# Rotary attention: the maximum and position term of four heads in one pass of 32-row products

## The reference, cut to what matters

```python
q = (x @ Wq).reshape(b, l, H, HD).transpose(0, 2, 1, 3)      # H = 16, HD = 64
k = (x @ Wk).reshape(b, l, KV, HD).transpose(0, 2, 1, 3)     # KV = 4, each for 4 heads
...
q = q * cos + _rotate_half(q) * sin
k = k * cos + _rotate_half(k) * sin
attn = jnp.einsum('bhqd,bhkd->bhqk', q, k) / math.sqrt(HD)
rel = (pos[None, :] - pos[:, None]).astype(x.dtype)
attn = attn + slopes[None, :, None, None] * rel[None, None, :, :]
attn = jax.nn.softmax(attn, axis=-1)
out = jnp.einsum('bhqk,bhkd->bhqd', attn, v)
...
return out @ Wo
```

## Time and profile before

| | before |
|---|---|
| median of three runs | 2129.33 us |
| the profiled execution | 2123.84 us |
| its span, first to last instruction | 2121.7 us |
| TensorE products busy | 1855.8 us (87%) |
| VectorE busy | 1319.6 us (62%) |
| ScalarE busy | 916.7 us (43%) |
| GpSimd (POOL) busy | 983.5 us (46%) |
| a batch of the rotary phase, 1497.29 to 1626.70 us | 129.41 us |

### The profile page before, as it was taken

The page is one execution under the profiler, slowest core; times in us unless marked ns, Lnnn a source line. Parts: engine busy times, 40 slices in busy tenths (PEclk is TensorE's granted clock), DMA queues, the critical chain, the costliest instruction groups (busy, mean ns, idle before and its releaser), DMA issues. The chain is left out here.

```text
span 2121.7 us, 36924 instructions
## 1 busy us (share of the span) xinstructions
PE 1855.8 (87%) x12145; PEld 1123.7 (53%) x12146; DVE 1319.6 (62%) x2902; ACT 916.7 (43%) x1313; POOL 983.5 (46%) x673
## 2 busy tenths in 40 slices
PE   5999999999997039999479999999999999999998
PEld 3454454454443038888445554645546465564654
DVE  3767767767765426666566565765657656566661
ACT  2656656656665114444224334242442524335152
POOL 2413233234244534444335737467373764737454
PEclk9999999999999569999879999999999999999999
DMA  5300000000010535555410010100101001010000
GB/s 174 129 6 6 10 0 10 10 0 10 0 60 40 193 115 183 192 191 196 118 31 2 1 41 1 41 1 10 33 1 41 2 11 32 1 41 1 11 21 11
DMA packets 56176, 104.86 MB, mean 49 GB/s; under 512 B 7238, under 2 KB 46566, under 8 KB 50156
## 3 DMA queue, kind: packets, MB, share of 16 engines
q1 hardware_dynamic: 52972, 94.71, 13.1%
q0 software_dynamic: 3072, 8.39, 1.2%
HBM read 76.35 MB, written 26.74 MB: 49 GB/s over the span
## 5 line engine op out<-in xcount | busy, mean ns | idle before, releaser
L369 POOL TENSOR_TENSOR a_probs<-a_probs 128x1024 f32<-128x1024 f32 x144 | 340.7, 2392 | 321.8 <-PE a_psO L696 321.8
L518 DVE CUSTOM_DVE_ANT_0 a_junk<-a_psM,a_alibi 128x512 bf16<-128x512 f32 x512 | 333.6, 688 | 208.8 <-PE a_psM L656 208.8
L1261 DVE TENSOR_REDUCE f_q_tok<-f_psR 128x1 f32<-128x512 f32 x512 | 323.1, 682 | 132.6 <-PE f_psR L1416 132.0
L452 ACT ACTIVATE a_probs<-a_psS 128x1024 f32<-128x1024 f32 x256 | 249.0, 1024 | 284.7 <-PE a_psS L682 284.6
L1199 ACT ACTIVATE f_probs<-f_psS 128x1024 f32<-128x1024 f32 x256 | 248.4, 1025 | 63.7 <-PE f_psS L1435 63.2
L696 PE MATMUL a_psO<-a_probs,a_v 128*32 128x512 f32 x2048 | 244.0, 597 | 0.0
L1416 PE MATMUL f_psR<-f_kP,f_qM 64*128 64x512 f32 x512 | 159.9, 493 | 25.7 <-DVE f_q_tok L1261 17.8
L656 PE MATMUL a_psM<-a_kH,a_qH 64*128 64x512 f32 x512 | 125.6, 486 | 43.8 <-DVE a_n_tok L518 37.5
L1822 ACT ACTIVATE e_h<-e_psH,w_o 128x256 f32<-128x256 f32 x152 | 63.9, 472 | 172.7 <-PE e_psH L1914 172.7
L1448 PE MATMUL f_psO<-f_probs,f_v 128*32 128x512 f32 x1024 | 136.4, 604 | 0.7 <-ACT f_probs L1199 0.6
L656 PEld LDWEIGHTS a_psM<-a_kH,a_qH 64*128 64x128 f32 x512 | 48.6, 186 | 157.3 <-DVE a_n_tok L518 107.4
(11 more groups left out here) (201 smaller groups left out, 3793.5 us busy)
## 6 DMA issues: line engine op xcount, KB each, us to landing
w_w_high<-w_parts SPq DMA_DIRECT2D x19, 1024.0 KB, 5.3
w_w_low<-w_parts SPq DMA_DIRECT2D x19, 1024.0 KB, 7.5
sorted_x<-f_zeros SPq DMA_DIRECT2D x1, 4864.0 KB, 19.9
e_xs<-sorted_x SPq DMA_DIRECT2D x19, 256.0 KB, 2.7
sorted_z<-e_z SPq DMA_DIRECT2D x19, 256.0 KB, 2.2
f_xn<-in_L_attn_x SPq DMA_DIRECT2D x8, 512.0 KB, 3.6
f_w_raw<-in_L_ffn_W SPq DMA_DIRECT2D x4, 1024.0 KB, 9.2
w_parts<-f_w_high SPq DMA_DIRECT2D x4, 1024.0 KB, 3.9
```

The source lines that it names most:

```text
L369: nc.gpsimd.tensor_tensor(slots, slots, probs[:, first - GRP:first - GRP + 2, :], ALU.add).then_inc(added.sem, 1)
L452: nc.scalar.activation(probs[:, slots, :], psS[:, 2 * p:2 * p + 2, :], ACT.Exp).then_inc(exp_done.sem, 1)
L518: nc.vector.tensor_tensor_reduce(out=junk[:, a, :], in0=psM[:, a, :], in1=alibi[:, h, :], scale=1.0, scalar=-3.0e38, op0=ALU.add, op1=ALU.max,
L1261: nc.vector.tensor_reduce(q_tok[:, c, h, NEG:NEG + 1], psR[:, ring_bank("max", u), :], AX.X, ALU.max, negate=True).then_inc(max_done.sem, 1)
```

## The change

The maxima of a whole quad are kept together. In n_tok a head e of the quad has its three columns (maximum, slope high, slope low) at column 32 e in place of 64 a for a pair, and one set of four transposes (99 rows) replaces two sets (67 rows): n 0 to 3 in place of n 0 to 7. qN has room for two quads in place of four pairs. The position products become one function, offsets, with four products of 32 rows each, at rows 0, 32, 64 and 96, one for each head and bank of psS. It starts the accumulation of all four banks, and scores adds the other three products of each. offsets is called at the start of the key tile, ahead of the early product for the maxima, and waits for the second exponential of the tile before and for all the side work read from the banks. The sets n that fall away in SIDE are those of (0,2), (1,2) and (2,2), and in PREPARE the one between two maxima; in the other places one set for the quad remains. At the start of the phase the constant rows are loaded and copied four times in place of two.

```diff
-    NR = 2 * QP
+    NR = 2
+    NW = P // GRP
+    NXR = (GRP - 1) * NW + 3
...
-                                                 ("max", 4), ("n", 0), ("out", 4), ("max", 5), ("q", 3), ("out", 4),
+                                                 ("max", 4), ("out", 4), ("max", 5), ("q", 3), ("out", 4),
                                                  ("max", 6), ("out", 4), ("max", 7), ("out", 4),
-                                                 ("max", 8), ("out", 4), ("n", 1)]
+                                                 ("max", 8), ("out", 4), ("n", 0)]
...
-    SIDE = {(0, 0): [("q", 4)], (0, 1): [("q", 5), ("k", 2)], (0, 2): [("n", 2), ("k", 3)], (0, 3): [("n", 3)],
-            (1, 0): [("q", 6)], (1, 1): [("q", 7)], (1, 2): [("n", 4), ("s", 0)], (1, 3): [("n", 5)],
-            (2, 2): [("n", 6), ("s", 1)], (2, 3): [("n", 7)],
+    SIDE = {(0, 0): [("q", 4)], (0, 1): [("q", 5), ("k", 2)], (0, 2): [("k", 3)], (0, 3): [("n", 1)],
+            (1, 0): [("q", 6)], (1, 1): [("q", 7)], (1, 2): [("s", 0)], (1, 3): [("n", 2)],
+            (2, 2): [("s", 1)], (2, 3): [("n", 3)],
...
-        n_tok = sb("n_tok", [P, PAIRS, HD + 3 * TT])
+        n_tok = sb("n_tok", [P, QUADS, (GRP - 1) * NW + 3 * TT])
...
-            for a in range(2):
-                sp.dma_start(const_rows[HD * a:HD * a + 3, :], key_rows).then_inc(staged, 16)
+            for e in range(GRP):
+                sp.dma_start(const_rows[NW * e:NW * e + 3, :], key_rows).then_inc(staged, 16)
...
-                    nc.scalar.copy(qN[0:XR, n % NR, :], psS[0:XR, bank, :]).then_inc(qN_done.sem, 1)
+                    nc.scalar.copy(qN[0:NXR, n % NR, :], psS[0:NXR, bank, :]).then_inc(qN_done.sem, 1)
...
+                    column = NW * (h % GRP) + 3 * c
...
-                        accum_out=n_tok[:, pair, HD * a + 3 * c:HD * a + 3 * c + 1]).then_inc(max_done.sem, 1)
+                        accum_out=n_tok[:, h // GRP, column:column + 1]).then_inc(max_done.sem, 1)
...
-                    pe.wait_ge(max_done.sem, max_done.at(b, 2 * (TT * n + TT - 1) + 1))
+                    pe.wait_ge(max_done.sem, max_done.at(b, 2 * (MQ * n + MQ - 1) + 1))
...
-                           "n": lambda: n_tok[:, n, 3 * t:3 * t + XR],
+                           "n": lambda: n_tok[:, n, 3 * t:3 * t + NXR],
...
-            def scores(b, quad, j, p, taken):
-
-                r, pair, keys = TT * quad + j, QP * quad + p, slice(j * P, (j + 1) * P)
-                needs = dict()
+            def offsets(b, quad, j, taken):
+
+                r, keys = TT * quad + j, slice(j * P, (j + 1) * P)
+                if r > 0:
+                    pe.wait_ge(exp_done.sem, exp_done.at(b, QP * (r - 1) + QP - 1))
+                else:
+                    pe.wait_ge(rot_sum.sem, rot_sum.at(b, NB - 1))
                 for kind, n in taken:
-                    needs[kind] = max(n, needs.get(kind, 0))
+                    pe.wait_ge(reader[kind].sem, reader[kind].at(b + 1 if kind == "x" else b, n))
                 if j == 0:
-                    needs["q"] = max(pair, needs.get("q", 0))
-                    needs["n"] = max(pair, needs.get("n", 0))
+                    pe.wait_ge(qN_done.sem, qN_done.at(b, quad))
+                for e in range(GRP):
+                    rows = slice(NW * e, NW * (e + 1))
+                    nc.tensor.matmul(psS[:, e, :], kN[rows, keys], qN[rows, quad % NR, :], start=True, stop=False,
+                                     tile_position=(NW * e, 0))
+
+            def scores(b, quad, j, p):
+
+                pair, keys = QP * quad + p, slice(j * P, (j + 1) * P)
+                if j == 0:
                     if p == 0:
-                        needs["k"] = max(quad, needs.get("k", 0))
-                if r > 0:
-                    pe.wait_ge(exp_done.sem, exp_done.at(b, QP * (r - 1) + p))
-                elif p == 0:
-
-                    pe.wait_ge(rot_sum.sem, rot_sum.at(b, NB - 1))
-                for kind, n in needs.items():
-                    pe.wait_ge(reader[kind].sem, reader[kind].at(b + 1 if kind == "x" else b, n))
-                products = ((kN[:, keys], qN[:, pair % NR, :]), (kH[:, quad, keys], qH[:, pair % QR, :]),
-                            (kH[:, quad, keys], qL[:, pair % QR, :]), (kL[:, quad, keys], qH[:, pair % QR, :]))
+                        pe.wait_ge(kL_done.sem, kL_done.at(b, quad))
+                    pe.wait_ge(qL_done.sem, qL_done.at(b, pair))
+                products = ((kH[:, quad, keys], qH[:, pair % QR, :]), (kH[:, quad, keys], qL[:, pair % QR, :]),
+                            (kL[:, quad, keys], qH[:, pair % QR, :]))
                 for n, (k, q) in enumerate(products):
                     for a, half in enumerate(SIDES):
-                        last = nc.tensor.matmul(psS[:, 2 * p + a, :], k[half], q[half], start=(n == 0),
+                        last = nc.tensor.matmul(psS[:, 2 * p + a, :], k[half], q[half], start=False,
                                                 stop=(n == len(products) - 1), tile_position=(HD * a, 0))
...
-                taken = {0: prepare_ring[-4:-2], 1: prepare_ring[-2:]}
+                taken = prepare_ring[-4:]
                 for quad in range(QUADS):
                     for j in range(TT):
                         r, items = TT * quad + j, side(quad, j, more)
                         early, late = maxima(quad, j)
+                        offsets(b, quad, j, taken)
                         if early is not None:
                             multiply_for_max(b, early)
                         for p in range(QP):
-                            scores(b, quad, j, p, taken.get(p, ()))
-                        taken = {0: items}
+                            scores(b, quad, j, p)
+                        taken = items
                         if late is not None:
                             multiply_for_max(b, late)
                         if items:

```

More of the change, by code:

```diff
@@ L26 @@
 GRP = H // KV
-XR = HD + 3
-XRP = XR + 1
 FH = D // H
@@ L204, in rotary_attention_phase @@
         w_low = ctx.enter_context(nc.semaphore("a_w_low"))
-        STAGED, LOADS, WO_LOADS = 6 * 16, 4 * 16, 2 * GRP * 16
+        STAGED, LOADS, WO_LOADS = 8 * 16, 4 * 16, 2 * GRP * 16
         x_in = sig("x_in", 1, step=16)
@@ L220, in rotary_attention_phase @@
         qL_done = sig("qL_done", PAIRS)
-        nT_ps = sig("nT_ps", PAIRS)
-        qN_done = sig("qN_done", PAIRS)
+        nT_ps = sig("nT_ps", QUADS)
+        qN_done = sig("qN_done", QUADS)
         max_ps = sig("max_ps", QUADS * MQ)
@@ L316, in _ @@
             for t in range(TT):
[L317 to L320, removed]
+                for e in range(GRP):
+                    first = NW * e + 3 * t + 1
+                    nc.gpsimd.tensor_copy(n_tok[:, :, first:first + 2], part_cols[:, e::GRP, :]).then_inc(slopes_set, 1)
+            pool.wait_ge(slopes_set, GRP * TT)
             def rotate(b, n):
@@ L405, in _ @@
             act.wait_ge(cleared, 3)
-            for a in range(2):
-                row = slice(HD * a, HD * a + 3)
+            for e in range(GRP):
+                row = slice(NW * e, NW * e + 3)
                 nc.scalar.copy(kN[row, :], const_rows[row, :]).then_inc(rows_made, 1)
@@ L469, in _ @@
             act.wait_ge(alibi_made, H)
-            act.wait_ge(slopes_set, 2 * TT)
+            act.wait_ge(slopes_set, GRP * TT)
             passes(act, batch)
@@ L592, in _ @@
             dve.wait_ge(alibi_made, H)
-            dve.wait_ge(slopes_set, 2 * TT)
+            dve.wait_ge(slopes_set, GRP * TT)
             dve.wait_ge(loads, LOADS)
@@ L616, in _ @@
             pe.wait_ge(ones_made, 1)
-            pe.wait_ge(rows_made, 2)
+            pe.wait_ge(rows_made, GRP)
             reader = {"proj": rot_half, "v": v_done, "k": kL_done, "q": qL_done, "n": qN_done, "x": xL_done,
@@ L640, in transpose @@
                            "q": lambda: q_tok[:, t, 2 * n:2 * n + 2, :].rearrange("p h d -> p (h d)"),
-                           "n": lambda: n_tok[:, n, 3 * t:3 * t + XR],
+                           "n": lambda: n_tok[:, n, 3 * t:3 * t + NXR],
                            "x": lambda: xn[:, t, n * P:(n + 1) * P]}[kind]()
-                    rows = XR if kind == "n" else P
+                    rows = NXR if kind == "n" else P
                     last = nc.tensor.transpose(psS[0:rows, bank, t * P:(t + 1) * P], src, idn[:, :])
```

## The result

| | before | after |
|---|---|---|
| median | 2129.24 us (4 runs) | 2160.40 us (4 runs, 2156.30 to 2163.71) |
| profiled span | 2121.7 us | 2159.9 us |
| TensorE products busy | 1855.8 us | 1867.9 us |
| a batch of the rotary phase, mean of batches 1 to 5 | 129.58 us | 133.54 us |

The change makes the kernel slower: 1.0148 times the time before (95% interval 1.0133 to 1.0163), 31 us. Batches count from 0. A batch, and a key tile, goes from its first product on TensorE to the first product of the next; so the batch from 1497.29 us before, whose end stands as 1626.70 in the table ahead of the prediction, ends at 1626.99 and takes 129.70 us.

The account below looks back on a forecast made before the run. TensorE and the chain early product, two maxima, late product were taken as tied at 2.1 us each. Terms summed to +3.57 us a batch, 28.6 in eight, +29.6 in all, about 2158 us; forecast 2157, range 2128 to 2180.

Parts of the forecast that it names:

- The chain and the change of shape: In nine key tiles a batch the early product and all behind come 0.45 us later, +4.05 us; shape change 0.21.
- rival B: Position products in key tiles: the four don't run side by side but as two pairs, 0.46 us; 2184 us; chance 0.08.
- Rival A: Key tiles: change between 32 and 64 rows is free, early product 0.34 us after T, load hidden; 2132 us; chance 0.22.
- Low parts and first tiles: Start of a batch: position products wait for low parts, +0.67 us in (0,1) to (0,3); (0,0) about +0.2 us.
- The further 0.18 and 0.12 us: In (0,2) and (0,3) the low part of k shifts with the late chain: +0.18 and +0.12 us.
- Transposes: Four of eight sets go, in (0,2), (1,2), (2,2) and among the projections: together -2.08 us a batch.
- The 0.39 us of the set among the projections: Between two products for the maxima, 2.74 us apart with the transposes and 2.35 without: 0.39 us saved a batch.
- The own range: Forecast case alone: 2146 us (change of shape at 0.15) to 2168 us (four position products at 0.30).
- A sign that was read wrongly in advance: Before the products for the maxima, idle time for VectorE was to rise from 37.5 to around 70 us.
- Rival C: Early product slips in under the 32-row pass, nine tiles cost nothing, transposes win; -18 us, 2111 us; chance 0.08.

Follow-up runs that it names:

- The runs with POOL's order: Only POOL's order in quad 2 changed, power of the variance ahead of normalising quad 0's outputs: 2118.62 us on the kernel before, 2155.50 us on the changed kernel.
- the last kernel: The changed kernel with, on POOL in quad 2, the power of the variance ahead of the normalisation of quad 0's outputs: 2155.50 us.

## Why the prediction was right

The forecast was 2157 us and +29.6 us (together they would be 2159); measured 2160.40 and +31.2. The terms for one batch beside the batches 1 to 5 of the two profiles, without the falls of the clock:

| tiles | forecast | measured |
|---|---|---|
| (0,0) and (0,1) | +1.02 us | +1.12 us |
| (0,2) and (0,3) | +0.67 | +0.48 |
| (1,0), (1,1), (1,3), (2,0), (2,1) | +2.25 | +2.05 |
| (1,2) | -0.13 | -0.20 |
| (2,2) | -0.58 | -1.29 |
| (2,3), (3,1), (3,2) | +0.69 | +0.63 |
| (3,0), (3,3) and on to the next batch | -0.35 | +0.25 |
| sum | +3.57 | +3.04 |

The falls add about 0.9 us a batch.

*The chain and the change of shape.* The delay was put at 0.45 us a tile. The start of the early product gives 0.43 (0.11 + q + 0.10, so q is about 0.22: the four products do run side by side, and rival B falls). The tiles (0,3), (1,0), (1,1), (1,3), (2,0), (2,1) grew by 0.36 to 0.47 us. Rival A's 0.34 and its hidden load are not there. That the place causes the delay is shown by the two kernels with 64-row products that differ in it (2155.52 and 2120.08 us). That a change of shape costs what one pass costs is shown by the 32 rows in the old place and by the 64 rows in the new one. The run with the early product first shows that the two don't add up: with the chain gone, two changes of shape in front of the exponential hold the tiles with transposes at the same length.

*Low parts and first tiles.* The position products wait for the low part of q in (0,1), as said, and +1.12 us came for +1.02. The further 0.18 and 0.12 us in (0,2) and (0,3) were mostly not there.

*Transposes.* Those behind the late products were worth what was said. The 0.39 us of the set among the projections was wrong: from the start of (3,3) to the first product of the next batch the batches take 0.28 us more, not 0.37 less. The position products, now first in the batch, wait for ScalarE's copy of the maxima: TensorE stands idle 1.36 to 1.80 us before the first product of the batches 1 to 6, where it was 0.74 to 1.04. The prediction gave the copies no price at that place. That is about 0.65 us a batch, some 4.5 us in seven, and with the early product first in (0,0) it is gone.

*What was left out, and cancelled.* The falls of the clock in (0,1) and (0,0) are about 7 us by the tiles' lengths, batch 0 included. In (2,2) the shorter wait for POOL gave back 0.7 us in seven batches, 5 us. The runs with POOL's order bear this out: that order was worth 10 us in the kernel before and 5 us in the changed one. So the closeness of 2157 to 2160 is luck in part; the mechanism and the size of its main terms are not.

*The own range.* Its ends, 2146 and 2168 us, do not follow from the two values named for them: 0.06 us in some 15 tiles of eight batches is 7 us, not 11.

*A sign that was read wrongly in advance.* L657's idle time for VectorE went from 37.5 to 43.8 us and not to 70. The missing 0.4 us a tile shows as 0.26, since the record of the product in front covers the rest, and the waits of (0,1) are now put down to the position products.

*Rival C* had the transposes right, but its condition failed: the early product does not slip in under the position pass, it starts 0.43 us behind it.

## What to carry to other kernels

Before work is moved ahead of an instruction, look what waits for that instruction: here 0.43 us put ahead of a product on which VectorE and the next product hang cost 0.4 us in most of nine tiles of sixteen, though TensorE had no more to do. Here a packing that saves a pass but needs another array shape saved nothing, since its neighbours have the old one; zeros in a second copy of the small operand kept the shape and still allowed the transposes to be merged. Moving one thing back does not give its price back when a second limit lies as high: look at the tiles, not at the total. When a gain does not come, look at which idle time on TensorE it lengthened or uncovered, and what the clock does behind it.

## What the runs showed of the hardware

- A change between 32-row and 64-row products cost 0.19 us, about half before the first product of the new shape and half between it and the next (0.42, 0.43 and 0.34 us against 0.34, 0.23 and 0.23). Four products of 32 rows side by side took about 0.22 us, an estimate (0.43 us from the position products to the early product, less 0.21 for the change), as one pair of 64 rows does (0.23).
- TensorE's granted clock fell to 0.50 (1.2 GHz) in the changed kernel behind idle times of 1.4 to 1.8 and 1.7 us close together, in two batches behind the first of them alone, and behind one of 2.14 us in the kernel with merged transposes. The same idle times did not decide it: the earlier trace rows's kernel waits 2.13 us in (2,2) and has no fall there, four of the batches 1 to 6 with 64 rows in the new place and two with POOL's order have none, while the kernel before with 32 rows has falls in (0,1) behind waits of no more than 1.1 us. A fall made its tile 0.6 to 1.7 us longer, and up to 3.2 us in two batches of the last kernel, where the clock stayed low for longer. In the four kernels in which one of the long waits was filled or shortened, the fall behind it did not come in any of the batches 1 to 6; the one with the early product first has falls elsewhere instead, in (2,2) of the batches 1 and 4.
- A TENSOR_SCALAR of 128x4 on VectorE took 1.72, 1.48, 1.01, 0.67 or 0.17 us, by when POOL's running 128x1024 product ended, within 0.03 us of which its record ends in all 56 cases of the eight profiles with the old order on POOL. The BATCH_NORM_AGGREGATE in front of it took 0.41 us beside POOL's product and without it, and L519, which reads one operand from PSUM, ran at 0.69 us beside POOL's work. The Trainium skill (GPSIMD Engine Reference, Specifications) has POOL's SBUF interfaces shared with VectorE, with contention for VectorE instructions in a 2-port perf mode or with two SBUF inputs. The runs agree that some operations are held up and others are not; whether this one is of the page's two kinds they don't show.
